# A four-stage transformer layer on one core: first group's keys made block-diagonal by TensorE, seven products on zeros, and a new order of all engines

## The reference

```
x = x + window_attention(layernorm(x))   # 16 heads of 8, 2 kv heads, blocks of 32 queries,
                                         # 64 keys per block, 32 of them inside each query's window
x = x + butterfly_ffn(layernorm(x))      # 128 -> 512, 9 butterfly stages, gelu, 9 stages, 512 -> 128
x = x + linear_attention(layernorm(x))   # phi = elu + 1, 16 heads, a kv state for each sequence
x = x + butterfly_ffn(layernorm(x))      # the same weights again
```

## Time and profile before

| | us |
|---|---|
| median of 3 runs | 568.12 (563.62, 568.12, 568.17) |
| the profiled execution | 568.07 |
| its span, first to last instruction | 566.3 |
| TensorE busy | 521.8 (92%) |
| GpSimd busy | 451.9 (80%) |
| VectorE busy | 436.6 (77%) |
| ScalarE busy | 352.2 (62%) |
| mean granted TensorE clock | 0.988 of full speed |

### The profile page before, as it was taken

One profiled execution on the slowest core, in us unless ns is written; L12 is line 12 of the kernel. 1 busy time (PEld: TensorE's weight loads), 2 busy tenths in 40 slices (PEclk: granted clock), 3 DMA queues, 4 the chain that ended last, 5 costly groups with the idle time before them and its releaser, 6 DMA issues.

```text
span 566.3 us, 14624 instructions
## 1 busy us (share of the span) xinstructions
PE 521.8 (92%) x5048; PEld 344.3 (61%) x5048; DVE 436.6 (77%) x1256; ACT 352.2 (62%) x570; POOL 451.9 (80%) x651
## 2 busy tenths in 40 slices
PE   3866888979999999999999999999999999999876
PEld 2623344546666676766667667566676767677654
DVE  7277979998898989889898888888988888664330
ACT  1323464755876767676776685876767676836632
POOL 6343788989898998999999989898998787877531
PEclk9969999998999999999999999999999999999999
DMA  8414233231222232222223232222222222100001
GB/s 312 139 46 99 62 79 89 59 80 44 68 69 65 58 77 69 68 69 70 71 71 77 68 79 68 63 68 65 57 71 58 69 56 66 39 20 20 2 20 37
DMA packets 50186, 39.14 MB, mean 69 GB/s; under 512 B 12480, under 2 KB 39616, under 8 KB 50112
## 3 DMA queue, kind: packets, MB, share of 16 engines
q1 hardware_dynamic: 47664, 33.99, 23.9%
q10 hardware_dynamic: 2448, 4.22, 2.1%
HBM read 15.89 MB, written 5.51 MB: 38 GB/s over the span
## 4 chain that ended last, share of the span: by engine, by line
PE 79%; DVE 8%; POOL 5%; issue 3%; ACT 2%; ACTq 2%; SPq 1%; DMA 0%; DVEq 0%; POOLq 0%
PE ring L563 20%; PE ring L575 18%; PE ps_s L531 9%; PE ring L512 6%; PE ring L586 5%; PE ps_o L548 4%; PE ring L606 4%; PE ring L646 3%; PE ring L623 2%; POOL probs_t L459 2%; PE ring L595 2%; PE ring L666 1%; DVE merged L1083 1%; PE ring L616 1%; DVE ps_s L1070 1%
## 5 line engine op out<-in xcount | busy, mean ns | idle before, releaser
L459 POOL TENSOR_TENSOR probs_t<-probs_t,first 128x1024 f32<-128x1024 f32 x64 | 151.5, 2368 | 10.8 <-DMA probs_t<-probs_t 10.8
L852 ACT ACTIVATE probs_t<-merged_t 128x1024 f32<-128x1024 f32 x64 | 67.1, 1048 | 54.2 <-DVE merged_t L1090 46.2
L833 ACT ACT_TABLE_LOAD x58 | 74.4, 1283 | 10.9 <-issue 9.8
L531 PE MATMUL ps_s<-kx,q_t 64*32 64x512 f32 x1024 | 71.5, 615 | 8.0 <-DVE merged L1083 5.3
L563 PE MATMUL ring<-xT_G,w1b 128*128 128x512 f32 x128 | 66.3, 608 | 1.7 <-ACT xT_G L821 1.6
L575 PEld LDWEIGHTS ring<-w,hid_G 128*128 128x128 f32 x512 | 59.5, 192 | 10.0 <-issue 6.7
L575 PE MATMUL ring<-w,hid_G 128*128 128x128 f32 x512 | 60.0, 275 | 1.7 <-ACT hid_G L843 1.7
L563 PE MATMUL ring<-xT_F,w1b 128*128 128x512 f32 x128 | 59.9, 611 | 0.4 <-ACT xT_F L821 0.4
L575 PE MATMUL ring<-w,hid_F 128*128 128x128 f32 x512 | 60.0, 275 | 0.0
L575 PEld LDWEIGHTS ring<-w,hid_F 128*128 128x128 f32 x512 | 58.6, 192 | 0.5 <-issue 0.4
L843 ACT ACTIVATE hid_G<-ring,b 128x512 f32<-128x512 f32 x64 | 43.5, 681 | 17.1 <-PE ring L563 17.1
(11 more groups left out here) (116 smaller groups left out, 1080.6 us busy)
## 6 DMA issues: line engine op xcount, KB each, us to landing
probs_t<-probs_t SPq DMA_DIRECT2D x256, 64.0 KB, 2.0
kx<-kv_rows SPq DMA_DIRECT2D x128, 40.0 KB, 2.2
x_P<-in_x SPq DMA_DIRECT2D x16, 256.0 KB, 3.3
out_x<-x_G SPq DMA_DIRECT2D x16, 256.0 KB, 2.4
vx_t<-kv_rows SPq DMA_DIRECT2D x128, 8.0 KB
up_s<-in_up_m ACTq DMA_DIRECT2D x7, 256.0 KB, 7.7
down_s<-in_down_m ACTq DMA_DIRECT2D x7, 256.0 KB, 7.7
kv_rows<-kv_t SPq DMA_DIRECT2D x16, 80.0 KB, 1.7
```

The source lines that it names most:

```text
L459: nc.gpsimd.tensor_tensor(parts, parts, keep.rearrange("p (a t) -> p a t", a=1).to_broadcast([P, PAIR * HEADS, WIN]), ALU.mult).then_inc(p ...
L531: last = nc.tensor.matmul(ps_s[32 * i:32 * i + 32, a], q_t[half, P * j + 32 * c:P * j + 32 * c + 32], kx[half, :, TSPAN * j + 32 * c:TSPAN ...
L833: nc.scalar.activation(unused[:, i:i + 1], half[0:1, 0:1], function)
L852: nc.scalar.activation(probs_t[:, j].rearrange("p s k h t -> p s (k h t)"), scores.to_broadcast([P, PAIR, HEADS * WIN]), ACT.Exp).then_inc ...
```

## The change

Four things are done.

1. **Keys of group 0 without DRAM.** TensorE multiplies group 0's `xT_P` by `wk_rep`, Wk with each column repeated for the eight heads (`X.ka`, `X.kb`: two products of 128x160 each). ScalarE writes the first half (8 ACTIVATEs of 128x288, one for each head, with a scale that is 1 on the head's own partitions and 0 elsewhere), VectorE the second half (8 TENSOR_SCALARs). They go to `kx_0`, a home of their own in the memory in which `hid_F` and `hid_G` lie later. So group 0 no longer loads `kx`, and group 1's load does not wait for group 0's scores. `kx` is cleared by GpSimd alone, the edges of `kx_0` too. `first` grows from 642 to 786 columns.
2. **Products on zeros.** Once `first` is in, TensorE makes seven products of 128x128 by 128x512 on `d_tmp`, which VectorE has zeroed, ahead of all else. VectorE's first use of `d_tmp`, the first outer stage of `w2`, waits for them.
3. **Loads.** The load of the ones for `vx_t` moves ahead to just behind `x` of group 1; `later` moves behind the values of group 0.
4. **Order.** All tables and all `turn` functions are new: the cycle of steps is another one, and some steps of group 0 and group 15 have a place apart from that of the other groups.

```diff
-FIRST = [("ident", P), ("last_half", WIN), ("keep", WIN), ("wq", P), ("wkv", 2 * KV * HD), ("bq", 1), ("bkv", 1), ("inside", TSPAN), ("bo", P)]
+FIRST = [("ident", P), ("last_half", WIN), ("keep", WIN), ("wq", P), ("wkv", 2 * KV * HD), ("bq", 1), ("bkv", 1), ("inside", TSPAN), ("bo", P), ("wk_rep", P), ("bk_head", HPK), ("head", HPK)]
...
-    ("W.S1", 4, "S"), ("W.PV1", 5, "T"), ("X.u2b", 3, "1", 0, 0), ("X.d5", 5, "3", 0, 0), ("X.u5b", 5, "3", 0, 0),
...
+    ("F.up3", 9, "1", 15, 15), ("F.up0", 9, "3"), ("X.u3b", 7, "2", 0, 0), ("F.up3", 9, "1", 0, 14), ("F.up1", 9, "2"),
...
-        hid = {s: sb(f"hid_{s}", [P, CH, TOK]) for s in "FG"}
+        early = sb("early", [P, HPK * TILES * TSPAN])
+        kx_0 = early[:].rearrange("p (h n) -> p h n", h=HPK)
+        hid = {s: early[:, CH * TOK * i:CH * TOK * (i + 1)].rearrange("p (c n) -> p c n", c=CH) for i, s in enumerate("FG")}
...
                     sp.dma_start(x_of(1, "P")[:], x_v[1]).then_inc(x_in[1], 16)
+                    sp.dma_start(vx_t[:], vones_c.rearrange("p (a n) -> p a n", a=1).to_broadcast([P, TILES, P])
+                                 ).then_inc(vones_in, 16)
...
                 sp.wait_ge(kv_out.sem, kv_out.after(g, "P.ko"))
-                sp.wait_ge(kx_cleared, 2)
-
-                sp.wait_ge(product.sem, product.after(g - 1, *SCORES))
+
+                if g == 1:
+                    sp.wait_ge(kx_cleared, 1)
+                else:
+                    sp.wait_ge(product.sem, product.after(g - 1, *SCORES))
...
-            nc.gpsimd.memset(kx[:, HPK // 2:], 0.0).then_inc(kx_cleared, 1)
+            for lo, hi in ((0, PAD), (2 * TSPAN - PAD, 2 * TSPAN + PAD), (TILES * TSPAN - PAD, TILES * TSPAN)):
+                nc.gpsimd.memset(kx_0[:, :, lo:hi], 0.0).then_inc(early_cleared, 1)
+            nc.gpsimd.memset(kx[:], 0.0).then_inc(kx_cleared, 1)
...
+            def first_keys(b):
+
+                name = f"X.k{'ab'[b]}"
+                drained_by(0, "P.xT", name)
+                free(0, name)
+                for i in range(TPB):
+                    last = nc.tensor.matmul(bank(name)[:, TSPAN * i:TSPAN * (i + 1)], wk_rep,
+                                            x_tp[:, b, P * i:P * i + TSPAN], start=True, stop=True)
+                last.then_inc(product.sem, 1)
...
             pe.wait_ge(first_in, 16)
+            pe.wait_ge(zeroed, 1)
+            for n in range(7):
+                last = nc.tensor.matmul(ring[3][:], d_tmp[:, 0], d_tmp[:].rearrange("p c n -> p (c n)"), start=True, stop=True)
+            last.then_inc(warmed, 1)
...
+                for h in range(HPK):
+                    last = nc.scalar.activation(kx_0[:, h, PAD:TPB * TSPAN - PAD], bank("X.ka")[:, PAD:TPB * TSPAN - PAD],
+                                                ACT.Identity, bias=bk_head[:, h:h + 1], scale=head_s[:, h:h + 1])
+                last.then_inc(drained[BANK["X.ka"]].sem, 1)
...
+                for h in range(HPK):
+                    last = nc.vector.tensor_scalar(kx_0[:, h, TPB * TSPAN + PAD:TILES * TSPAN - PAD],
+                                                   bank("X.kb")[:, PAD:TPB * TSPAN - PAD], head_s[:, h:h + 1],
+                                                   bk_head[:, h:h + 1], ALU.mult, ALU.add)
+                last.then_inc(drained[BANK["X.kb"]].sem, 1)
...
                     dve.wait_ge(d_in, 16)
+                    dve.wait_ge(warmed, 1)
...
-            nc.vector.memset(kx[:, 0:HPK // 2], 0.0).then_inc(kx_cleared, 1)
+            nc.vector.memset(d_tmp[:], 0.0).then_inc(zeroed, 1)
```

More of the change, by code:

```diff
@@ new lines, in turn @@
+                for g in due(t, 10, 0, 14):
+                    linear_out(g, 0)
+                for g in due(t, 7):
+                    scores(g, 3)
+                if t == 7:
+                    up_stage(4, "b")
+                for g in due(t, 8):
+                    weighted_values(g, 2)
+                if t == 7:
+                    up_stage(4, "a")
+                    up_stage(5, "a")
+                if t == 5:
+                    attention_q(0)
+                if t == 4:
+                    norm_transposed(0, "P", "P")
+                    up_stage(1, "a")
@@ new lines, in turn @@
+                for g in due(t, 11):
+                    norm_transposed(g, "G", "L")
+                if t == 6:
+                    scores(0, 0)
+                if t == 27:
+                    ffn_up(15, "G", 3)
+                for g in due(t, 9):
+                    ffn_down(g, "F")
+                if t == 25:
+                    linear_out(15, 0)
+                    linear_out(15, 1)
+                for g in due(t, 6, 1, 15):
+                    attention_q(g)
+                if t == 8:
+                    down_stage(4)
@@ new lines, in turn @@
+                for g in due(t, 8, 1, 15):
+                    weighted_values(g, 3)
+                if t == 8:
+                    heads_transposed(0)
+                for g in due(t, 6, 1, 15):
+                    scores(g, 0)
+                for g in due(t, 11, 0, 14):
+                    ffn_up(g, "G", 1)
+                if t == 7:
+                    up_stage(6, "a")
+                    up_stage(5, "b")
+                if t == 29:
+                    ffn_down(15, "G")
+                if t == 4:
+                    first_keys(0)
@@ new lines, in turn @@
+                for g in due(t, 5, 1, 15):
+                    attention_q_out(g)
+                for g in due(t, 10, 0, 14):
+                    gelu(g, "G", 2)
+                for g in due(t, 4, 1, 15):
+                    keys_input_out(g)
+                for g in due(t, 10, 0, 14):
+                    gelu(g, "G", 3)
+                if t == 7:
+                    down_stage_out(4)
+                if t == 24:
+                    copy_out(15, "L.oT", o_lt[:], "L.proj")
+                if t == 6:
+                    down_stage_out(3)
@@ L938, in turn @@
+                if t == 3:
+                    first_keys_out()
+                for g in due(t, 10, 0, 14):
+                    gelu(g, "G", 1)
+                for g in due(t, 7):
+                    copy_out(g, "W.oT", o_wt[:], "W.proj")
+                for g in due(t, 10):
+                    gelu(g, "G", 0)
+                for g in due(t, 9, 0, 14):
+                    copy_out(g, "L.oT", o_lt[:], "L.proj")
                 for g in due(t, 8):
-                    linear_q_parts(g)
@@ new lines, in turn @@
+                for g in due(t, 3):
+                    subtract_max(g, 3)
+                for g in due(t, 5):
+                    residual(g, "F", "F.down", "W")
+                    moments(g, "F")
+                for g in due(t, 4):
+                    head_outputs(g, 3)
+                for g in due(t, 3):
+                    values_out(g)
+                for g in due(t, 6):
+                    linear_normalised(g, 1)
+                for g in due(t, 3):
+                    scores_transposed(g, 3)
@@ L1190, in turn @@
+                for g in due(t, 2):
+                    merge_halves(g, 0)
+                    row_max(g, 0)
+                for g in due(t, 4, 1, 15):
+                    residual(g, "W", "W.proj", "P")
+                for g in due(t, 2):
+                    subtract_max(g, 0)
+                if t == 4:
+                    residual(0, "W", "W.proj", "P")
+                for g in due(t, 4):
+                    moments(g, "W")
                 for g in due(t, 6):
                     residual(g, "L", "L.proj", "F")
-                for g in due(t, 4):
-                    residual(g, "W", "W.proj", "P")
@@ L1220, in turn @@
-                for g in due(t, 5):
-                    phi_q_made(g)
                     linear_state_out(g)
```

556 lines of the change are left out of this document (280 added, 276 removed), and 56 rows, old and new, of tables (COVERED, PRODUCTS, VECTOR).

## The result

The changed kernel takes **564.1 us** (median of 17 runs, 562.42 to 566.11) against 568.12 for the kernel before in the same comparison (17 runs): the ratio is 0.9934, with a 95% interval of [0.9918, 0.9949]. That is 4.0 us faster, where 7.1 were forecast. The profiled execution has a span of 561.5 us (563.48 in all).

What follows compares the result with a forecast made beforehand. TensorE's own work was taken to bound full turns, leaving 44.5 us idle, at the ends, and low-clock time to win. Terms -8.2 + 2 - 1 + 0 = -7.2 from 568.07 gave 561 us, own range 558 to 564, wider range 554 to 570.

Steps and rivals of the forecast that it cites:

- group 1's first scores: Start of the kernel: group 1's first scores start at 39.1 us instead of 48.28, 9.2 earlier.
- work undone at them: At group 1's first scores TensorE has done less of other steps' work, 1.0 us, leaving net -8.2.
- full turns: Eleven full turns of the middle: a stall of 0.2 us a turn around the `o_l` transposes, +2 us.
- fill, with `X.wT` moved: First turns: may run closer as `X.wT`, 3.6 us, leaves group 1's turn; 0 to -3, taken as -1 us.
- tail: From `L.kv` of group 15 on: same steps, 7.6 us from `L.proj` to last transpose; 0, between -1.5 and +1.
- Group 0's first scores: Start of the kernel: zeros end at 14.5 us, group 0's first scores start at 23.4 instead of 27.76.
- The keys' stall in groups 2 to 4: Groups 2 to 4: keys take 7.9 us, scores 6.8 apart; 1 us stall each, hidden in idle time, taken as 0.
- stays low: Rival at the start: the clock stays low through the zero products, which take 12.4 us; 565.5 us, chance 0.12.
- The fill gives it back: Rival in the fill: group 1 starts earlier but VectorE paces the fill; 566.7 us, chance 0.18.
- The slower rival: Rival in the full turns: waits on GpSimd for VectorE's moments add 1.2 us a turn; 574 us, chance 0.13.
- The fill runs closer: Rival: no stall in the turn and 3 us won from the moved work; 555 us, chance 0.10.

Runs made afterwards that it cites:

- Run 1: The changed kernel without its seven products on zeros and without VectorE's wait for them: 561.0 us, ratio 0.9875 to the kernel before.
- runs 4: The changed kernel, but group 1's key load waits for group 0's last scores again: 566.71 us, ratio 0.9982 to the kernel before.
- run 5: The changed kernel with group 0's keys by way of DRAM again, without key products, their copies and kx_0: 573.26 us, ratio 1.0093 to the kernel before.
- runs 9: The changed kernel without zeros, ScalarE's key copies in halves with the queries between, kx cleared before group 0's norm: 566.12 us, ratio 0.9960 to before.
- 10: On top of 9, the down stages' loads on SyncE's queue and group 0's transpose ahead of the second up stage: 565.65 us, ratio 0.9952 to before.
- 11: On top of 9, three products with unread results in TensorE's idle stretches before group 1's third and fourth scores: 565.24 us, ratio 0.9957 to before.

## Why the prediction was right, and where it was not

The sum by its own terms, with what the profiles of before and after show (differences between single executions, so a few tenths each are noise):

| term | predicted | measured |
|---|---|---|
| group 1's first scores | -9.2 | -7.55 |
| work undone at them | +1.0 | +1.0 (counted) |
| full turns | +2 (eleven) | +1.7 (ten turns) |
| fill, with `X.wT` moved | -1 | -0.7 (what is left up to `F.up` of group 15, 516.39 to 510.86) |
| tail | 0 | +0.7 |
| sum | -7.2 | -4.8 |

- **Group 0's first scores**: right in its steps, 24.20 for 23.4. The zeros took 9.34 for 8.4 (their passes are 0.85 us apart up to 11.81 and 0.45 behind it, so three and a half products were slow and not two and a half), but `first`, wider as it is, had landed at 5.67 and not 6.1, and `xT_P`'s copy came at 17.22, ahead of the forecast 17.6. The lateness is ScalarE's: eight key copies took 3.97, where I had 3.2. The failing part is what the sum took for granted: that the warmth of the zeros returns what they delay. It gave TensorE's start 5.4 us away for it, and never costed the keys' path without them. Run 1 shows 3 us.
- **Group 1's first scores**: 39.1 forecast, 40.73 measured; this is the step that failed most. 0.8 came along from group 0. VectorE was 0.5 faster than I took it: `ps_s` was empty at 39.39, 4.4 us after the last scores began, not 4.9. And I let the scores start there, and forgot what TensorE must issue first in its own order: `P.q` (38.30), a down stage and the next group's transpose (40.14), which cost 1.3 behind it.
- **Full turns**: the size was right by luck. The transposes of `o_l`, where I had put a stall of 0.2 us a turn, average 287 ns instead of 273, 0.06 us a turn, and those of `xn_L` the same. As a whole an undisturbed turn is 0.08 longer (30.31 against 30.23), 0.8 in ten. The two turns with the wait for the store of `out_x` add 1.5, on which the forecast had no term; before has three longer turns of its own (30.40 to 30.68), 0.9 over its plain ones, without such a wait.
- **The keys' stall in groups 2 to 4**: taken as 1 us each, hidden in idle time. The first scores of these groups wait 0.39, 0.47 and 0.17 us, marked "issue", each up to within 0.1 us of when the eighth key load is due (2.2 us after its issue); before, 0.45 at group 2. It does not show as a longer fill.
- **The tail**: the steps from `L.proj` of group 15 to its last transpose take 7.17 us (7.58 before), and are nearly as fixed as forecast. But the clock fell near the end (0.77 granted from 548 to 555 us), and the last `G.up` runs at 5.23 us where before it took 3.70 (timelines, after and then before):

```profile
548.07 5.23 PE L589 MATMUL ring<-xT_G,w1b 128*128 128x512 f32 x8 [0.75 <-ACT xT_G L896]
```

```profile
554.31 3.70 PE L563 MATMUL ring<-xT_G,w1b 128*128 128x512 f32 x8 [0.75 <-ACT xT_G L821]
```

- **Rivals.** The clock did rise within the zeros (a pass takes 1223 ns at the start, 592 at the end), so "stays low" is out. What the Trainium skill, page TensorE: Matmul & The Clock Gate, "Seeing it yourself", says of zero operands and the peak current does not carry over to the clock: here it rose while they ran. "The fill gives it back" is out by runs 4 and 5. The slower rival is out as GpSimd's pace, by the undisturbed turns of 30.31; two turns of 31.15 and 31.00 did come, with a DMA as the first cause. "The fill runs closer": not seen beyond -0.7. Its time was also summed wrongly: no stall (2) and the 2 left of the 3 us from the moved work give 557, not 555.

What the 4 us rest on, then: the order, the zeros and the moved loads together cost 5.1 us (run 5 against before), the keys' part gives back 9.2 (run 5 against after). Without the zeros the whole gives 7.1 (run 1), by chance the number that was forecast with them.

## What to carry to other kernels

Price a new order at one milestone per phase (here: the first scores of groups 1, 5 and 15) and count the work undone at each; a start that is 7.5 us earlier in a deeper order was worth 4. Before warming TensorE up with idle products, ask whether the clock would have risen over the useful chain by the time they end, since the chain stands behind them in order. When a step of the start is split or moved, look at which bank its successor waits for: runs 9, 10 and 11 had the first scores' queries and keys ready before 20.4 us, where run 1 has them, and started the scores 3 to 4 us later than it, behind a bank that a stage of another chain shared. And look for a store whose buffer is written again soon: here most landed in time, and two in ten turns held VectorE up.

## What the runs showed of the hardware

- Fourteen identical passes (seven products of 128x512) on zeros from 5.4 to 5.9 us on took 7.67, 9.05, 9.09 and 9.34 us in four profiles: the moment at which the clock rises varies, and moves such a start by up to 1.7 us.
- Sharing between VectorE and GpSimd went beyond `memset`: `down_outer_stage`'s four scalings (L302) take 0.87 us, but 3.26 without zeros (and 3.27 before), where they run beside GpSimd's 4 us of `up_diag`:

```profile
9.17 4.03 POOL L465 TENSOR_TENSOR up_diag<-first,up_mix 128x512 f32<-128x512 f32 x4
...
10.21 3.26 DVE L302 TENSOR_SCALAR d_tmp<-d_t,outer 128x128 f32<-128x128 f32 x4
```

- Eight ACTIVATEs of 128x288 with a scale and a bias per partition take 3.97 us, eight of 128x144 still 3.00: half the columns save a quarter.
